# A Perceiver block on one core: self-attention of the first layer on row and column groups of the array, its softmax bank by bank, and the router's gates behind the first expert's products

## The chip, the cores and the metric

The kernel runs on one core of a Trainium2 chip. The metric is the device time in microseconds (us) of one execution, as the median of repeated runs. Engines are named as in the profile: PE is TensorE (PEld its weight loads), DVE is VectorE, ACT is ScalarE, POOL is GpSimd, SP is SyncE, which issues the DMAs. TensorE's clock has two levels, 1.2 and 2.4 GHz; the profile shows them as a granted clock of 0.50 and 1.00, called the lower and the upper level below.

## The reference, cut to what matters

128 tokens of width 256 pass through two layers. Each layer has cross-attention to 12,544 context rows, self-attention or a stand-in for it, and a mixture of experts. The change lies in the first layer, from the end of its cross-attention to its experts:

```python
x = x + cross_attention(layernorm(x), ctx)      # 16 heads of 16, then relu(out @ W1 + b1) @ W2 + b2
# self-attention, 16 heads of 16
q, k, v = split(layernorm(x) @ c_attn_w + c_attn_b)
w = q @ k.T / sqrt(16)                           # per head
w = softmax(where(causal, w, -1e10))
x = x + (w @ v) @ c_proj_w + c_proj_b
# 8 experts, the two best by softmax(x @ Wg + bg)
for e in range(8):
    x = x + (gelu(xn @ W1[e] + b1[e]) @ W2[e] + b2[e]) * w_e
```

## The kernel before, in words

Each engine runs its own list of instructions in the order in which the code issues them; waits on semaphores tie the lists together. `Settle` is a helper that makes DVE wait for its own last instruction. Nothing is planned at run time.

The first cross-attention walks the context twice: a first pass with 14 chunks of 896 rows makes keys, values and a maximum per query, a second pass with 98 steps scores, exponentiates and weighs. The second pass already uses column groups of the array: `weigh0` writes 32 columns of output at PSUM partitions 32*i for i in 0..3, 16 products to a step. The first pass uses row groups of 64: `score_pair` takes partitions 0 to 63 and 64 to 127 of its operands by turns.

Then comes a stage in which one engine after another works on 128 x 256 values (lines 916 to 981 of `tensor`, 1215 to 1228 of `scalar`, 1502 to 1546 of `vector`). `att` is transposed (`PE_AT`), DVE adds a bias (`D_AT`), PE makes the hidden layer (`PE_HID`), DVE its relu (`D_HID`), PE the output and its bias row (`PE_FFN`), DVE adds it to x. A layernorm follows (DVE, with one operation on POOL), its transpose (PE) and a copy (ACT, `xnT`). Self-attention projects queries and keys (`PE_QK`) and values (`PE_V`). DVE adds biases and spreads each query over the 128 partitions with a mask (`D_SPREAD`, 128 x 2048), so that each head's scores are one product over all 128 rows, of which 16 hold its query. PE puts the causal mask into a bank as a product with the identity and adds four heads' scores to it, four times (`PE_SC`). DVE takes one maximum over all heads and subtracts it (2048 columns each), ACT exponentiates all 2048 columns (`A_EXP`), PE transposes 16 heads, ACT and DVE copy a half each (`A_PT`, `D_PT`). PE then weighs with the probabilities as stationary operand and 16 columns of values as moving one (`PE_AV`), DVE multiplies by the reciprocal of the sums, PE transposes, ACT copies, PE projects (`PE_PR`).

The router (`gate`, 16 short DVE operations and one exponential) comes after the next layernorm. PE waits for it, turns the gates, waits for the copy on ACT, forms the gated bias `b2`, and only then starts `hidden0(0)`. The expert loop alternates `hidden0(e)` (16 products of 128 columns) and `down0(e-1)` (8 of 256). A loader on SP brings expert e+4 once expert e is summed.

Matrix products whose operands are float32 show as two records each in the profile. `mm` and DVE's and ACT's helpers put most records on the helper's line (L692, L1287, L1288, L1291, L1091), so groups are told apart by tile and shape. `q_all` in a row is also the scratch space of this stage.

Of the kernel before, what the change touches and what calls it, by code (L numbers as in the profile page):

```python
# [7 lines left out]
F32 = mybir.dt.float32  # L8
F16 = mybir.dt.float16
ALU = mybir.AluOpType  # L10
# [31 lines left out]
def perceiver_kernel(nc, d, out):  # L42
# [18 lines left out]
    with ExitStack() as ctx:  # L61
# [21 lines left out]
        cp = tail[:, 272:784].rearrange("p (a n) -> p a n", a=2)  # L83
        bias_rows = tail[0:8, 784:784 + D]
        wv16 = sb("wv16", [P, 4, 1024], F16)
        v16 = sb("v16", [P, 2 * 8 * 130], F16)
        W = sb("W", [P, 15680], F32)
# [17 lines left out]

        def dram(name, shape, dt=F16):
            return nc.dram_tensor(name, shape, dt, kind="Internal").ap()
# [5 lines left out]
        ld_ctx = [sem(f"ld_ctx{n}") for n in range(3)]  # L113
        ld_keys = [sem(f"ld_keys{n}") for n in range(2)]
# [4 lines left out]
        COLS_IN, TAIL_IN, GATE_IN = 6 * 16, 14 * 16, 16 * 16  # L119
# [28 lines left out]
        tail_blank = sem("tail_blank")  # L148
# [232 lines left out]
        qkT = scratch[:, 0:512].rearrange("p (a q) -> p a q", a=4)  # L381
        v_tok = scratch[:, 512:768]
        sa_spread = scratch[:, 768:768 + 2048].rearrange("p (h q) -> p h q", h=H)
        sa_probT = scratch[:, 768:768 + 2048].rearrange("p (h q) -> p h q", h=H)
        sa_prob = scratch[:, 2816:2816 + 2048].rearrange("p (h q) -> p h q", h=H)
# [10 lines left out]
        PE_AT, PE_HID, PE_FFN, PE_QK, PE_V, PE_SC, PE_PT, PE_AV, PE_AT2, PE_PR = range(1, 11)  # L396
        PE_WT, PE_B2, PE_WO, PE_VS, PE_VT, PE_VY = range(11, 17)
        A_VTOK, A_EXP, A_PT, A_AT2, A_WT, A_VEXP, A_VT = range(1, 8)
        D_AT, D_HID, D_SPREAD, D_CENTRED, D_PT, D_ATT, D_VCEN, D_VROWS = range(1, 9)


        def sync(sp):
# [95 lines left out]
            load_blocks(ld_bias, tail[:, 272:784], d["L0_attn_c_proj_w"])  # L498
# [7 lines left out]
            load_blocks(ld_w2, W[:, CA_OFF:], d["L0_attn_c_attn_w"])  # L506

# [182 lines left out]
        def tensor(pe):  # L690
# [231 lines left out]
            ins.then_inc(step_pe, 1)  # L922
            pe.wait_ge(step_dve, D_AT)
# [4 lines left out]
            ins.then_inc(step_pe, 1)  # L928
            pe.wait_ge(step_dve, D_HID)
            for f in range(4):  # L930
                mm(ps[:, 2, 0:D], ff_hT[:, f, :], w2[:, f, :], f == 0, False)
            mm(ps[:, 2, 0:D], row_select("L0_xattn_b2"), bias_rows, False, True).then_inc(step_pe, 1)


            turn_xn(1, 0)
            ca = wview(CA_OFF, 2, 3 * D)
            pe.wait_ge(ln_made, 2)
            for n in range(4):
                for a in range(2):
                    ins = mm(ps[:, 1, n * P:(n + 1) * P], ca[:, a, n * P:(n + 1) * P], xnT[:, a, :], a == 0, a == 1)  # L940
            ins.then_inc(step_pe, 1)
            for a in range(2):
                mm(ps[:, 2, 0:D], xnT[:, a, :], ca[:, a, 2 * D:3 * D], a == 0, False)
            mm(ps[:, 2, 0:D], row_select("L0_attn_c_attn_b"), bias_rows, False, True).then_inc(step_pe, 1)
            pe.wait_ge(step_dve, D_SPREAD)
            for b in range(4):
                mm(ps[:, 4 + b, :], ident[:, :], bc(causal[:, :], 1, [P, 4, P]), True, False, skip_group_check=True)
                for j in range(4):
                    h = 4 * b + j
                    ins = mm(ps[:, 4 + b, j * P:(j + 1) * P], sa_spread[:, h, :], qkT[:, 2 + h // 8, :], False, True,  # L950
                             skip_group_check=True)
            ins.then_inc(step_pe, 1)
            pe.wait_ge(step_act, A_EXP)
            for h in range(H):
                ins = pe.transpose(ps[:, h // 4, (h % 4) * P:(h % 4 + 1) * P], sa_prob[:, h, :], ident[:, :])
            ins.then_inc(step_pe, 1)
            pe.wait_ge(step_act, A_PT)
            pe.wait_ge(step_dve, D_PT)
            for h in range(H):
                ins = mm(ps[:, 4, h * 16:(h + 1) * 16], sa_probT[:, h, :], v_tok[:, h * 16:(h + 1) * 16], True, True)  # L960
            ins.then_inc(step_pe, 1)
            pe.wait_ge(step_dve, D_ATT)
            for i in range(2):
                ins = pe.transpose(ps[:, 5, i * P:(i + 1) * P], att[:, i * P:(i + 1) * P], ident[:, :])
            ins.then_inc(step_pe, 1)
            pe.wait_ge(step_act, A_AT2)
            for a in range(2):
                mm(ps[:, 6, 0:D], sa_attT[:, a, :], cp[:, a, :], a == 0, False)
            mm(ps[:, 6, 0:D], row_select("L0_attn_c_proj_b"), bias_rows, False, True).then_inc(step_pe, 1)


            turn_xn(2, 0)
            pe.wait_ge(ln_made, 3)
            for a in range(2):
                mm(ps[:, 1, 0:NE], xnT[:, a, :], wg[:, a, :], a == 0, False)
            mm(ps[:, 1, 0:NE], row_select("L0_ffn_bg"), bias_rows[:, 0:NE], False, True).then_inc(gate_in, 1)
            pe.wait_ge(gate_made, 1)
            pe.transpose(ps[0:8, 2, 0:P], g_w, ident[:, :]).then_inc(step_pe, 1)
            pe.wait_ge(step_act, A_WT)
# [658 lines left out]
```

## Time and profile before

| | |
|---|---|
| median of 3 runs | 1517.76 us (1512.5 to 1522.74) |
| the profiled execution, its own time | 1513.2 us |
| its span | 1511.5 us |
| PE busy / DVE busy / ACT busy | 1386.6 / 1042.2 / 1062.0 us |
| mean granted TensorE clock | 0.966 |
| second pass of the first cross-attention ends | 462.2 us |
| stage that the change touches | 462.2 to 586.8 us |

Times in the rows are microseconds from the start of the span. A timeline row gives start, duration from the first start to the last end, engine, line, operation, output <- inputs, shape, how many instructions, and in brackets how long the engine stood idle before it and what ended that.

### The profile page before, as it was taken

The page shows a single profiled execution, that of the slowest core. Times are in us where ns is not written, and L with a number is a line of the kernel's source. Part 1 is how long each engine was busy: PE and PEld are TensorE (multiplying, and loading weights), DVE is VectorE, ACT ScalarE, POOL GpSimd, SP SyncE. Part 2 cuts the span into 40 slices and gives each one's busy share as a digit, 9 for nine tenths or more (in the row PEclk, how much of TensorE's full clock was granted, in tenths as well). Part 3 has the DMA queues.
Part 4 walks back from the last instruction along what each step waited for, and adds up shares of the span by engine and source line. Part 5 has one row for each costly group of instructions (what it writes and reads, how often), then busy time and mean ns, then how long its engine had stood idle before and what let it go on. Part 6 is the DMA issues. An engine that isn't in the chain of part 4 may idle for free.

```text
span 1511.5 us, 36970 instructions
## 1 busy us (share of the span) xinstructions
PE 1386.6 (92%) x15312; PEld 921.4 (61%) x15312; DVE 1042.2 (69%) x1482; ACT 1062.0 (70%) x1630; POOL 106.4 (7%) x145
## 2 busy tenths in 40 slices
PE   5888887999997598999999979999998999989969
PEld 2444444777775497433333447777776777767758
DVE  6999997000002302999999998888888888887842
ACT  4787776999992133666666658888887888877820
POOL 6232220000000002200000000000000000000000
PEclk9999999999998599999999989999999999999979
DMA  4445437676656054555654567777777677797630
GB/s 138 157 183 185 168 121 200 155 181 148 170 127 223 1 196 136 191 183 201 229 192 179 188 148 147 147 146 146 147 139 146 123 147 143 147 258 136 158 125 4
DMA packets 128794, 236.48 MB, mean 156 GB/s; under 512 B 9244, under 2 KB 114166, under 8 KB 128630
## 3 DMA queue, kind: packets, MB, share of 16 engines
q1 hardware_dynamic: 128630, 234.13, 58.2%
q8 instruction: 122, 2.00, 0.6%
q14 instruction: 42, 0.34, 0.1%
HBM read 155.98 MB, written 78.12 MB: 155 GB/s over the span
## 4 chain that ended last, share of the span: by engine, by line
PE 61%; DVE 21%; issue 11%; ACT 2%; DMA 2%; SPq 2%; POOL 0%; POOLq 0%; DVEq 0%; ACTq 0%
PE ps L692 60%; DVE W L1291 6%; DVE small L1354 5%; DVE p L1291 5%; DMA W<-keys_hi 1%; SPq L405 1%; ACT W L1114 1%; DMA W<-in_ctx_dram 1%; DVE W L1321 1%; DVE q_all L1291 1%; SPq L463 0%; ACT p L1128 0%; DVE ctxT_b L1343 0%; DVE att L1291 0%; DVE ctxT_a_lo L1347 0%
## 5 line engine op out<-in xcount | busy, mean ns | idle before, releaser
L1291 DVE TENSOR_TENSOR p<-ps,p 128x512 f16<-128x512 f32 (+1 forms) x467 | 350.5, 751 | 70.2 <-ACT ps L1091 67.5
L1091 ACT ACTIVATE p<-ps 128x512 f16<-128x512 f32 (+1 forms) x490 | 329.2, 682 | 90.2 <-PE ps L692 88.0
L692 PEld LDWEIGHTS ps<-q_all,W 128*128 128x128 f16 (+1 forms) x3544 | 230.9, 99 | 69.7 <-issue 17.3
L692 PE MATMUL ps<-q_all,W 128*128 128x128 f16 (+2 forms) x3544 | 264.2, 227 | 9.1 <-DMA W<-keys_hi 6.1
L1354 DVE TENSOR_REDUCE small<-ps 128x1 f32<-128x896 f32 x224 | 241.4, 1079 | 4.7 <-PE ps L692 4.3
L1091 ACT ACTIVATE ps<-ps 128x512 f32<-128x512 f32 x392 | 235.8, 602 | 0.0
L692 PE MATMUL ps<-v,p 128*128 128x130 f16 x3136 | 169.7, 206 | 5.4 <-DVE p L1291 3.3
L692 PE MATMUL ps<-wv,ctxT_a_hi 128*128 128x512 f16 (+1 forms) x588 | 155.3, 346 | 10.3 <-DVE W L1321 6.1
L692 PEld LDWEIGHTS ps<-v,p 128*128 128x128 f16 x3136 | 147.4, 97 | 12.2 <-ACT ps L1091 3.6
L692 PE MATMUL ps<-wv,ctxT_b 128*128 128x512 f16 (+1 forms) x588 | 154.5, 344 | 0.0
L1291 DVE TENSOR_TENSOR v<-ps,v 128x512 f16<-128x512 f32 x196 | 135.4, 691 | 15.6 <-ACT v L1186 2.9
L1411 DVE COPY att<-ps 128x512 f32<-128x512 f32 x1 | 0.7, 692 | 204.4 <-PE ps L692 204.4
L692 PE MATMUL ps<-ctxT_a_hi,q_all 128*128 128x448 f16 (+1 forms) x464 | 126.3, 356 | 0.6 <-DVE p L1291 0.6
L692 PE MATMUL ps<-ctxT_b,q_all 128*128 128x448 f16 (+1 forms) x464 | 125.1, 353 | 0.0
L692 PE MATMUL ps<-W,q_all 64*128 64x448 f16 (+1 forms) x684 | 105.4, 363 | 19.1 <-DVE small L1354 6.6
L1116 ACT CAST p<-ps 128x896 f16<-128x896 f32 x75 | 68.0, 906 | 61.0 <-PE ps L692 61.0
L692 PE MATMUL ps<-wv,ctxT_a_lo 128*128 128x512 f16 (+1 forms) x294 | 101.3, 344 | 0.0
L1091 ACT ACTIVATE W<-ps 128x1024 f32<-128x1024 f32 x98 | 95.0, 1021 | 7.4 <-PE ps L692 5.1
L1128 ACT CAST p<-ps 128x896 f16<-128x896 f32 x104 | 92.9, 907 | 9.9 <-PE ps L692 8.9
L692 PEld LDWEIGHTS ps<-wv,ctxT_b 128*128 128x128 f16 x588 | 57.6, 98 | 48.9 <-issue 0.8
L692 PE MATMUL ps<-ctxT_a_lo,q_all 128*128 128x448 f16 (+1 forms) x240 | 82.7, 354 | 0.0
L692 PEld LDWEIGHTS ps<-W,q_all 64*128 64x128 f16 (+1 forms) x684 | 35.7, 108 | 70.6 <-issue 38.7
(226 smaller groups left out, 1744.8 us busy)
## 6 DMA issues: line engine op xcount, KB each, us to landing
W<-keys_hi SPq DMA_DIRECT2D x54, 896.0 KB, 14.6
W<-keys_low SPq DMA_DIRECT2D x27, 896.0 KB, 11.7
keys_hi<-p SPq DMA_DIRECT2D x75, 224.0 KB, 2.0
keys_low<-p SPq DMA_DIRECT2D x75, 224.0 KB, 1.9
keys_hi<-W SPq DMA_DIRECT2D x65, 224.0 KB, 2.0
keys_low<-W SPq DMA_DIRECT2D x65, 224.0 KB, 2.0
W<-values SPq DMA_DIRECT2D x14, 960.0 KB, 9.2
W<-in_L_ffn_W_dram SPq DMA_DIRECT2D x10, 1024.0 KB, 8.8
```

The lines of the kernel that those rows point to most:

```text
L405: sp.dma_start(by_rows(region, a, n), src.rearrange("(a p) n -> p a n", p=P)).then_inc(s, 16)
L692: return pe.matmul(out_, lhsT, rhs, start=start, stop=stop, **kw)
L1091: return act.activation(out_, in_, ACT.Exp, scale=scale)
L1114: ins = act.activation(dst, src, ACT.Identity, bias=bk_scaled[:, i:i + 1])
L1116: ins = act.copy(dst, src)
L1128: act.copy(dst.rearrange("p (n k) -> p n k", n=MAXB), src).then_inc(max_copied, 1)
L1291: return dve.tensor_tensor(out_, a, b, op)
L1321: ins = dve.scalar_tensor_tensor(out=low, in0=src, scalar=bk_scaled[:, i:i + 1], in1=hi, op0=ALU.add, op1=ALU.subtract)
L1354: dve.tensor_reduce(mpart[:, among(L, h), n:n + 1], ps[:, 2 * pair:2 * pair + 2, 0:MAXC], AX.XY, ALU.max).then_inc(max_reduced, 1)
L1411: dve.tensor_copy(att[:, 512:1024], ps[:, O0_BANK, :]).then_inc(outT_made, 1)
```

## The change

Order of PE's list and what it computes with:

- The four causal products leave the score loop: they are issued behind the transposes of `att`, behind the hidden layer, and two behind the FFN output. The bias rows of the FFN output, of the value projection, of the output projection and of the router's logits are issued ahead of the wait that their product had, as the first of the group.
- Queries and keys go to two banks. DVE writes each query twice, scaled by 0.25 and by `quarter`, a 0/0.25 mask of every other 16 rows (`q_half`); ACT adds the keys' bias (`kT`). Scores are products over 32 partitions, four row groups by turns, each into its own bank.
- The softmax goes bank by bank: DVE maximum and subtraction of 512 columns, ACT exponential of 512, PE four transposes, ACT (three banks) or DVE (the last) copy of 512.
- The values (32 columns of `v_tok`, the last 16 rows of zeros from a memset) are the stationary operand, the probabilities the moving one, over four column groups, like `weigh0`; a same set with a block of ones before it gives the sums, spread over the partitions. DVE takes the reciprocal of 128 x 512 sums. The result is already transposed, so the transposes, their copy and the separate scaling are gone. The projection takes four products with a `cp` that is zero in every other 16 rows. It lies in the space of `wv16`, blanked by DVE and loaded by four DMAs behind the loads of the FFN's weights.
- The gates' transpose is issued behind `hidden0(0)`, the gated bias behind `hidden0(1)`; ACT copies the gates behind the first expert's gelu.

```diff
+            def add_causal(r):
+                mm(ps[:, 4 + r, :], ident[:, :], bc(causal[:, :], 1, [P, 4, P]), True, False, skip_group_check=True)
+            add_causal(0)
             pe.wait_ge(step_dve, D_AT)
...
+            mm(ps[:, 2, 0:D], row_select("L0_xattn_b2"), bias_rows, True, False)
+            add_causal(1)
             pe.wait_ge(step_dve, D_HID)
...
+            add_causal(2)
+            add_causal(3)
             turn_xn(1, 0)
+            mm(ps[:, 2, 0:D], row_select("L0_attn_c_attn_b"), bias_rows, True, False)
             pe.wait_ge(ln_made, 2)
...
-            pe.wait_ge(step_dve, D_SPREAD)
-            for b in range(4):
-                mm(ps[:, 4 + b, :], ident[:, :], bc(causal[:, :], 1, [P, 4, P]), True, False, skip_group_check=True)
-                for j in range(4):
-                    h = 4 * b + j
-                    ins = mm(ps[:, 4 + b, j * P:(j + 1) * P], sa_spread[:, h, :], qkT[:, 2 + h // 8, :], False, True,
+            pe.wait_ge(step_dve, D_Q)
+            pe.wait_ge(step_act, A_K)
             for a in range(2):
+                for j in range(2):
+                    for r in range(4):
+                        rows, n = slice(32 * r, 32 * (r + 1)), 2 * a + j
+                        ins = mm(ps[:, 4 + r, n * P:(n + 1) * P], q_half[rows, j, a, :], kT[rows, a, :], False, True,
...
+            for r in range(4):
+                pe.wait_ge(sa_exped, r + 1)
+                for n in range(4):
+                    ins = pe.transpose(ps[:, r, n * P:(n + 1) * P], sa_prob[:, 4 * r + n, :], ident[:, :])
+                ins.then_inc(sa_turned, 1)
+            pe.wait_ge(sa_copied, 3)
+            pe.wait_ge(step_dve, D_PT)
+            for bank in (4, 5):
+                for k in range(4):
+                    for i in range(4):
+                        h = 4 * k + i
+                        lhsT = ones32 if bank == 4 else v_tok[:, h * 16:h * 16 + 32]
+                        ins = mm(ps[32 * i:32 * (i + 1), bank, k * P:(k + 1) * P], lhsT, sa_probT[:, sa_slot(h), :],
+                                 True, True)
+                ins.then_inc(step_pe, 1)
+            mm(ps[:, 6, 0:D], row_select("L0_attn_c_proj_b"), bias_rows, True, False)
+            pe.wait_ge(ld_cp, 64)
+            pe.wait_ge(step_dve, D_ATT)
+            for k in range(4):
+                ins = mm(ps[:, 6, 0:D], sa_out[:, k * P:(k + 1) * P], cp[:, k, :], False, k == 3)
...
-            pe.wait_ge(gate_made, 1)
-            pe.transpose(ps[0:8, 2, 0:P], g_w, ident[:, :]).then_inc(step_pe, 1)
-            pe.wait_ge(step_act, A_WT)
-            mm(ps[:, 1, 0:D], wT, bias2, True, True).then_inc(step_pe, 1)
...
                 if e < NE:
                     hidden0(e)
+                if e == 0:
+                    pe.wait_ge(gate_made, 1)
+                    pe.transpose(ps[0:8, 0, 0:P], g_w, ident[:, :]).then_inc(step_pe, 1)
+                if e == 1:
+                    pe.wait_ge(step_act, A_WT)
+                    mm(ps[:, 1, 0:D], wT, bias2, True, True).then_inc(step_pe, 1)
                 if e:
                     down0(e - 1)
...
+            act.wait_ge(step_pe, PE_K)
+            for a in range(2):
+                ins = act.activation(kT[:, a, :], ps[:, 3, a * P:(a + 1) * P], ACT.Identity,
+            for r in range(4):
+                act.wait_ge(sa_centred, r + 1)
+                own = sa_prob[:, 4 * r:4 * (r + 1), :]
+                exp(own, own).then_inc(sa_exped, 1)
+                if r:
+                    act.wait_ge(sa_turned, r)
+                    act.copy(sa_probT[:, 4 * (r - 1):4 * r, :].rearrange("p n q -> p (n q)"), ps[:, r - 1, :]).then_inc(sa_copied, 1)
...
+                dve.wait_ge(values0_out, 4 * NCH)
+                dve.memset(cp, 0.0).then_inc(cp_blank, 1)
...
+            for a in range(2):
+                for j in range(2):
+                    ins = ts(q_half[:, j, a, :], ps[:, 1, a * P:(a + 1) * P], col("L0_attn_c_attn_b", a),
+                             quarter[:, j:j + 1], ALU.add, ALU.mult)
...
+            for r in range(4):
+                scores = ps[:, 4 + r, :].rearrange("p (n q) -> p n q", n=4)
+                own = mx[:, 4 * r:4 * (r + 1)]
+                settle(dve.tensor_reduce(own, scores, AX.X, ALU.max))
+                tt(sa_prob[:, 4 * r:4 * (r + 1), :], scores, bc(own, 2, [P, 4, P]), ALU.subtract).then_inc(sa_centred, 1)
+            dve.wait_ge(sa_turned, 4)
+            dve.tensor_copy(sa_probT[:, 12:16, :].rearrange("p n q -> p (n q)"), ps[:, 3, :]).then_inc(step_dve, 1)
+            dve.wait_ge(step_pe, PE_SUM)
+            settle(dve.reciprocal(per_sum, ps[:, 4, :]))
+            dve.wait_ge(step_pe, PE_AV)
+            tt(sa_out, ps[:, 5, :], per_sum, ALU.mult).then_inc(step_dve, 1)
```

PE's list from the transposes of `att` to the first expert; `causal` is the mask, `stage,ident` a bias row, `q_all` stands for the scratch. Before:

```order
L921 MATMUL ps<-ident,att 128x128 x2
L692 MATMUL ps<-q_all,W 128x128 x8
L692 MATMUL ps<-W,q_all 128x256 x4
L692 MATMUL ps<-stage,ident 128x256
L696 MATMUL ps<-ident,xn 128x128
L697 MATMUL ps<-ident,xn 128x128
L692 MATMUL ps<-xnT,W 128x128 x8
L692 MATMUL ps<-W,xnT 128x256 x2
L692 MATMUL ps<-stage,ident 128x256
L692 MATMUL ps<-causal,ident 128x512
L692 MATMUL ps<-q_all 128x128 x4
```

and in the changed kernel:

```order
L936 MATMUL ps<-ident,att 128x128 x2
L707 MATMUL ps<-causal,ident 128x512
L707 MATMUL ps<-q_all,W 128x128 x8
L707 MATMUL ps<-stage,ident 128x256
L707 MATMUL ps<-causal,ident 128x512
L707 MATMUL ps<-W,q_all 128x256 x4
L707 MATMUL ps<-causal,ident 128x512 x2
L711 MATMUL ps<-ident,xn 128x128
L712 MATMUL ps<-ident,xn 128x128
L707 MATMUL ps<-stage,ident 128x256
L707 MATMUL ps<-xnT,W 128x128 x8
L707 MATMUL ps<-W,xnT 128x256 x2
```

The mask stands in three places ahead of the scores, and each bias row ahead of its products.

PE's list from the weighing to the first expert's products (`small` holds the block of ones and the gates, `wv` the projection's weights). Before:

```order
L692 MATMUL ps<-q_all 128x16 x16
L964 MATMUL ps<-ident,att 128x128 x2
L692 MATMUL ps<-stage,q_all 128x256 x2
L692 MATMUL ps<-stage,ident 128x256
L696 MATMUL ps<-ident,xn 128x128
L697 MATMUL ps<-ident,xn 128x128
L692 MATMUL ps<-stage,xnT 128x8 x2
L692 MATMUL ps<-stage,ident 128x8
L978 MATMUL ps<-ident,small 8x128
L692 MATMUL ps<-stage,q_all 128x256
L692 MATMUL ps<-xnT,stage 128x128 x16
```

and in the changed kernel:

```order
L707 MATMUL ps<-q_all,small 32x128 x16
L707 MATMUL ps<-q_all,att 32x128 x16
L707 MATMUL ps<-stage,ident 128x256
L707 MATMUL ps<-wv,q_all 128x256 x4
L711 MATMUL ps<-ident,xn 128x128
L712 MATMUL ps<-ident,xn 128x128
L707 MATMUL ps<-stage,ident 128x8
L707 MATMUL ps<-stage,xnT 128x8 x2
L707 MATMUL ps<-xnT,stage 128x128 x16
L1042 MATMUL ps<-ident,small 8x128
```

The gates' transpose has moved behind the 16 products of the first expert.

## Rows read from the trace of the kernel before

**Rows 1.** The page: the chain that ended last, shares of the span by engine
```profile
PE 61%; DVE 21%; issue 11%; ACT 2%; DMA 2%; SPq 2%; POOL 0%; POOLq 0%; DVEq 0%; ACTq 0%
```

**Rows 2.** Stretches: from:to, length, PE busy (x records), granted clock, DMA share, GB/s
```profile
465.00:475.00 10.00, 8.08 (x27) 0.50 1.06 383
479.00:482.00 3.00, 2.99 (x14) 0.52 1.04 382
482.00:495.00 13.00, 9.18 (x50) 1.00 0.14 44
496.00:533.00 37.00, 23.48 (x91) 0.50 0.00 1
533.00:587.00 54.00, 53.80 (x362) 1.00 0.56 190
```

**Rows 3.** Timeline, FFN output to the scores
```profile
462.26 0.69 DVE L1411 COPY att<-ps 128x512 f32<-128x512 f32 x1 [204.43 <-PE ps L692]
466.00 3.78 PE L692 MATMUL ps<-q_all,W 128*128 128x128 f32 x16 [0.70 <-DVE q_all L1287]
471.00 3.78 PE L692 MATMUL ps<-W,q_all 128*128 128x256 f32 x8 [1.22 <-DVE q_all L1288]
475.59 0.42 DVE L1291 TENSOR_TENSOR x_tok<-ps,x_tok 128x256 f32<-128x256 f32 x1 [4.65 <-PE ps L692]
479.01 3.40 PE L692 MATMUL ps<-xnT,W 128*128 128x128 f32 x16 [0.46 <-ACT xnT L1095]
486.03 1.12 PE L692 MATMUL ps<-causal,ident 128*128 128x512 f32 x2 [2.13 <-DVE q_all L1291]
486.99 1.05 PE L692 MATMUL ps<-q_all 128*128 128x128 f32 x8
```

**Rows 4.** Timeline, softmax to the projection
```profile
493.34 2.29 DVE L1531 TENSOR_REDUCE small<-ps 128x16 f32<-128x2048 f32 x1 [7.36 <-PE ps L692]
499.95 3.68 PE L955 MATMUL ps<-ident,q_all 128*128 128x128 f32 x16 [6.65 <-ACT q_all L1091]
505.11 6.98 PE L692 MATMUL ps<-q_all 128*128 128x16 f32 x32 [1.48 <-DVE q_all L1538]
517.01 0.42 DVE L1291 TENSOR_TENSOR x_tok<-ps,x_tok 128x256 f32<-128x256 f32 x1 [4.46 <-PE ps L692]
```

**Rows 5.** Timeline, the router and the first experts
```profile
520.59 1.02 PE L692 MATMUL ps<-stage,xnT 128*128 128x8 f32 x4 [0.46 <-ACT xnT L1095]
525.68 0.23 DVE L1287 TENSOR_SCALAR small<-small 128x8 f32<-128x8 f32 x1
527.84 6.32 PE L692 MATMUL ps<-xnT,stage 128*128 128x128 f32 x32
541.03 3.73 PE L692 MATMUL ps<-xnT,W 128*128 128x128 f32 x32
544.60 3.62 PE L692 MATMUL ps<-W,q_all 128*128 128x256 f32 x16
```

**Rows 6.** Groups by shape: busy us, mean ns of one; ACT, DVE, reciprocals
```profile
L1091 ACT ACTIVATE ps<-ps 128x512 f32<-128x512 f32 x392 | 235.8, 602 | 0.0
L1291 DVE TENSOR_TENSOR q_all<-ps,q_all 128x512 f32<-128x512 f32 x8 | 5.5, 691 | 24.0 <-PE ps L692 24.0
L1431 DVE RECIPROCAL small<-small 128x3 f32<-128x3 f32 x4 | 0.7, 176 | 0.1
L1416 DVE RECIPROCAL small<-small 128x16 f32<-128x16 f32 x1 | 0.3, 253 | 0.0
```

**Rows 7.** Timeline: column groups in the second pass, row groups in the first
```profile
445.52 0.81 PEld L692 LDWEIGHTS ps<-W 128*32 128x32 f32 x32 [0.21 <-issue]
445.52 1.08 PE L692 MATMUL ps<-W 128*32 128x128 f32 x32
120.86 0.11 PEld L692 LDWEIGHTS ps<-W,q_all 64*128 64x128 f16 x4 [0.37 <-DVE W L1321]
120.86 0.55 PE L692 MATMUL ps<-W,q_all 64*128 64x448 f16 x4
```

More of the change, by code:

```diff
@@ L104, in perceiver_kernel @@
         bk_scaled = small[:, 234:236]
+        quarter, ones32 = small[:, 48:50], small[:, 64:96]
         def dram(name, shape, dt=F16):
@@ L935, in tensor @@
+            add_causal(2)
+            add_causal(3)
             turn_xn(1, 0)
             ca = wview(CA_OFF, 2, 3 * D)
+            mm(ps[:, 2, 0:D], row_select("L0_attn_c_attn_b"), bias_rows, True, False)
             pe.wait_ge(ln_made, 2)
-            for n in range(4):
-                for a in range(2):
-                    ins = mm(ps[:, 1, n * P:(n + 1) * P], ca[:, a, n * P:(n + 1) * P], xnT[:, a, :], a == 0, a == 1)
+            for bank, first in ((1, 0), (3, 2)):
+                for n in range(2):
+                    w = slice((first + n) * P, (first + n + 1) * P)
+                    for a in range(2):
+                        ins = mm(ps[:, bank, n * P:(n + 1) * P], ca[:, a, w], xnT[:, a, :], a == 0, a == 1)
+                ins.then_inc(step_pe, 1)
@@ L956, in tensor @@
-            ins.then_inc(step_pe, 1)
[L957 to L965, printed above, removed]
@@ L976, in tensor @@
[L976 to L980 removed]
+                ins = mm(ps[:, 1, 0:NE], xnT[:, a, :], wg[:, a, :], False, a == 1)
+            ins.then_inc(gate_in, 1)
             def hidden0(e):
@@ L1194, in attend1 @@
                             exp(bank, bank, 1.0 / VS).then_inc(exped, 1)
-            def copy_attT(n, dst, bank, value):
-                nb = -(-n // 4)
-                w = min(n, 4) * P
-                act.wait_ge(step_pe, value)
-                return act.copy(dst.rearrange("p (b i) q -> p b (i q)", b=nb), ps[:, bank:bank + nb, 0:w])
             def gate(k, second):
@@ L1441, in attend0 @@
                 first_pass(L0)
+                dve.wait_ge(values0_out, 4 * NCH)
+                dve.memset(cp, 0.0).then_inc(cp_blank, 1)
+                settle(dve.tensor_reduce(quarter, head16[:, :].rearrange("p (a j) -> p j a", j=2), AX.X, ALU.add))
+                ts(quarter, quarter, 0.25, None, ALU.mult)
+                dve.memset(ones32, 1.0)
                 normalise0()
@@ L1517, in vector @@
             layernorm(1)
-            dve.wait_ge(step_pe, PE_QK)
-            for n in range(4):
-                ins = ts(qkT[:, n, :], ps[:, 1, n * P:(n + 1) * P], col("L0_attn_c_attn_b", n),
-                         0.25 if n < 2 else 1.0, ALU.add, ALU.mult)
-            settle(ins)
-            for i in range(2):
-                ins = tt(sa_spread[:, 8 * i:8 * i + 8, :], bc(qkT[:, i, :], 1, [P, 8, P]),
-                         bc(head16[:, :], 2, [P, 8, P]), ALU.mult)
+            dve.memset(v_tok[:, D:D + 16], 0.0)
@@ L1526, in vector @@
+            dve.wait_ge(step_pe, PE_Q)
+            for a in range(2):
+                for j in range(2):
+                    ins = ts(q_half[:, j, a, :], ps[:, 1, a * P:(a + 1) * P], col("L0_attn_c_attn_b", a),
+                             quarter[:, j:j + 1], ALU.add, ALU.mult)
             ins.then_inc(step_dve, 1)
-            mx, tot = small[:, 16:32], small[:, 32:48]
-            sch = ps[:, 4:8, :].rearrange("p b (j q) -> p b j q", j=4)
-            mx4 = mx.rearrange("p (b j) -> p b j", b=4)
+            mx = small[:, 16:32]
```

80 lines of the change are left out of this document (35 added, 45 removed).

## The prediction

> **What bounds the kernel now.** I read the chain of waits first: by engine PE holds 61% of it, DVE 21%, "issue" 11% [rows 1]. Over the whole span that says little about this change, so the next view is the stage itself, 462.2 to 586.8 us. In the chain's order of time every piece there follows the one before within 0.02 to 0.14 us, on alternating engines: nothing overlaps until the first expert. So here each microsecond taken from the chain comes off the time. The timeline gives the pieces: FFN [rows 3], scores [rows 3], softmax, weighing and projection [rows 4], router [rows 5]. Then the stretches with the granted clock [rows 2]: 0.50 from 465 to 475, 1.00 from 482 to 495, 0.50 from 496 to 533, 1.00 in the experts. At the lower level a float32 product of 256 columns costs 3.78/4 = 0.95 us, at the upper 3.62/8 = 0.45; one of 128 columns 3.40/8 = 0.42 mostly at the lower, 3.73/16 = 0.23 at the upper [rows 3, 5]. The clock rose after PE had worked without a pause for some 3 to 6 us (from 471.0 it rose by 475, from 479.0 by 482, from 527.8 at 533), and it was low again in the stage wherever PE mostly waited.
>
> **The change, term by term** (times of before in brackets; negative is gain).
>
> a) To the FFN's residual [its wait ends at 475.59]. The first mask product begins as the last transpose of `att` streams, 0.9 us before the hidden layer's 466.00. Masks cost 486.99 - 486.03 = 0.96 us each at the upper level [rows 3], twice that at the lower. The wait for DVE was only 0.70 us, so the hidden layer starts about 1 us later than 466.00. But PE now has no gap from 464.7 on; I expect the clock to rise some 3 to 4 us in, which makes the hidden layer's 3.78 about 2.6 and ends it near 469.5 (before 469.78). DVE's relu takes 1.13; under it go the bias row (0.45) and the second mask (0.96), about as long. The four output products cost 4 x 0.45 = 1.8 plus 0.1 to drain: residual at 472.6. **-3.0**. Of this, 0.84 is the bias row off the path, the rest the clock.
>
> b) To the first score product [475.59 to 486.03, masks not counted]. Layernorm to xn is unchanged, 2.5 us, and covers masks three and four (1.9 at the upper level, 3.6 at the lower). Transposes and the copy to xnT 0.9; the value bias row hides under the copy. Then PE runs 8 products of 128 columns (8 x 0.23 = 1.9) and 2 of 256 (0.9). Queries are ready halfway: DVE's four operations (1.1) end before the values do, and ACT's two (0.37 each, as its copies of 256 columns) with them. What goes: the wait for the queries' bias behind all eight products and the spread over 128 partitions, 2.4 us of DVE. 2.5 + 0.9 + 1.9 + 0.9 = 6.2 against 10.4. **-4.2**.
>
> c) Scores [486.03 to 493.32, 7.3]. Masks gone: 4 x 0.9. The 16 products took 16 x 0.23 = 3.6. In row groups they fall between two bounds. Above: nothing overlaps, 3.6. Below: four groups at once, 3.6/4 = 0.9 plus a drain of 0.15. The nearest row is the first pass's two groups of 64: four products of 448 columns took 0.55 us, where one alone streams 0.187, and their four weight loads took 0.11 together [rows 7]. Both loads and products overlap there, so I take 1.05. **-6.2**. The Trainium skill, "TensorE: Matmul & The Clock Gate", Part 3, gives 3.07x for four row groups; by it this would be 3.6/3.07 = 1.2 us, an estimate. No row here has four row groups or float32 ones.
>
> d) Softmax to the first weighing product [493.34 to 505.11, 11.8]. DVE does per bank a maximum and a subtraction, each a quarter of 2.29 with its fixed part, 0.62 [rows 4], at most 0.69 [rows 6]; the fourth bank is centred after 8 x 0.64 = 5.1 us, 0.5 more than now. But ACT (0.60 + 0.60 per bank [rows 6]) and PE (four transposes 3.68/4 = 0.92 at the lower level [rows 4]) keep pace with its 1.28. After the fourth: exponential 0.6, transposes 0.95, DVE's copy 0.69, hand-offs 0.1: 7.45 in all. **-4.3**. The sum over probabilities and its reciprocal of 16 (2.5 us on DVE) were hidden by PE and don't count.
>
> e) Weighing to the residual [505.11 to 517.01, 11.9]. Before, 6.98 for 16 products of 16 columns (at the lower level, bound by weight loads), scaling 0.44, transposes 0.70, copy 0.38, projection 3.2. Now two sets of 16 in column groups: 1.08 each at the upper level, the very form of the second pass [rows 7], 2.15 at the lower. The reciprocal of 128 x 512 is on the path behind the first set. From 3 to 16 columns it rises 77 ns, 5.9 ns a column [rows 6], so 512 cost 3.2; a bound below is 0.69, as any operation on 512 [rows 6]. I take 3.2, since the slope is measured on the same instruction; it hides the second set. Scaling 0.69, four products 3.7 or 1.9. 2.15 + 3.2 + 0.7 + 3.7 + 0.15 = 9.9 at the lower level, 8.1 if the weighing, over 4 us without a pause, lifts the clock. I take 9.0. **-2.9**. The Trainium skill, "VectorE: DVE Perf Modes", in the walkthrough of the pipeline's modes, says that a reciprocal repeats its divide step 8 times, at 0.96 GHz; by it 512 columns would be 4.3 us, an estimate, and the time 1.1 us longer. The slope of the rows is less.
>
> f) Router [520.59 to 527.84, 7.25]. Now the experts' products follow the logits' four records (1.0) at once. DVE's gates, whose last operation ends 525.91 - 521.61 = 4.3 us behind them [rows 5], lie beside the first 16 products, 6.3 at the lower level and 3.7 at the upper: no or next to no wait. The gates' transpose (0.25) and the gated bias (0.45) now stand between full products. -6.25 + 0.7 = **-5.5**. The copy of the gates on ACT is due while `hidden0(1)` runs, after the first gelus; covered.
>
> Edits at nothing: `memset`s, `quarter` and the blanking of `cp` fall into the 204 us in which DVE waits for the second pass [rows 3]; the four small loads go out 200 us before their use, and SP's wait for the blanking ends before the next keys are wanted. The loads that run at 479 to 482 (DMA share 1.04) are the weights of experts 1 and 3; they are nearly over in the next stretch (0.14) [rows 2], and needed from about 508. Later loads are released by the experts themselves and move along, as all behind does.
>
> **Sum**: 3.0 + 4.2 + 6.2 + 4.3 + 2.9 + 5.5 = 26.1 us. On the profiled execution's 1513.2 that is 1487.1; the median shown is 4.6 higher, so 1491.7. I forecast **1491**.
>
> A switch of the array's form may cost too. In the second pass, which switches twice a step, the weight loader stands 0.21 us at each switch [rows 7], and PE doesn't show it. The Trainium skill, "TensorEngine Tiling (Array Packing)", Key Properties, says that changing the mode drains TensorE; by it the four new switches would add about 4 x 0.2 = 0.8 us, an estimate with the row's length.
>
> **Rivals.**
> 1. *The clock stays at the lower level until the scores.* For: from 465 to 475 PE was busy for 8.08 of 10 us and the clock stayed there [rows 2]. Against: the two rises that came within 4 us. Then a) is +1.3 (a mask of 1.9 in a gap of 0.7, mask and bias row of 2.8 in one of 1.2, less the bias row), b) -1.8, c) -5.2, e) -2.0: gain 17.5, time 1500. Chance 0.15.
> 2. *Float32 row groups don't overlap*, by loads of 128 columns each. c) is -3.7, the time 1494. Chance 0.13.
> 3. *Hand-offs eat it*: the softmax ping-pong waits at every bank and the change is within 1%. That needs 11 us more than worked out, on some 30 hand-offs of 0.02 to 0.14 us each. Chance 0.04.
> 4. *Slower: the experts run at the lower level.* Before, the clock rose only after 5 us of unbroken products from 527.84. Now the experts start from the same low clock, with a wait for the gates that could break the run. An expert costs 7.0 us at the upper level [rows 5], twice that at the lower. To eat 26 us and cost 15 more, six of eight experts would have to run low: 1517.8 + 16 = 1534. Against it: PE had no pause of a microsecond in its 54 us [rows 2]. Chance 0.02.
>
> The forecast itself keeps 0.66. The range takes in the cheap reciprocal and a clock that is high throughout (-2.5, -2.5, and 3 for the spread of runs) and the first rival: **1483 to 1502**. A measurement tells about 1% from no change, 15 us; below 1502.6 is faster. All of forecast and rival 2, and two thirds of rival 1, lie there: faster 0.89, same 0.09, slower 0.02.
>
> **What would show it.** Hidden layer ends within 0.5 us of where it did and the FFN's products take under 2 us; 16 score products in a little over 1 us; the sums' reciprocal near 3.2 us, with PE idle behind the weighing for it; x's second residual some 20 us earlier; first expert's products within 1 us of the logits; experts as long as before. I am wrong if scores take over 3 us, if the clock shows 0.50 from 465 to the scores, if the softmax takes over 9 us from scores to weighing, or if the stretches outside the stage change length.

## The result and the profile after

The changed kernel takes 1493.39 us (median of 4 runs, 1491.6 to 1495.53) against 1516.15 for the kernel before (the median of four runs now; of the first three it was 1517.76): ratio 0.9848, 95% interval 0.9824 to 0.9872, 22.8 us less. The profiled execution's span went from 1511.5 to 1490.9 us, by 20.6. The forecast was 1491, the range 1483 to 1502. Two executions of kernels further down, 1631.39 us of the one with only the gates' part and 3298.05 us of the one with products in the stage, were slow ones and stand in no ratio.

Timeline of the changed kernel, attention output to the first score's maximum; columns as in [rows 3]:

```profile
467.63 0.44 PE L936 MATMUL ps<-ident,att 128*128 128x128 f32 x2 [1.01 <-DVE att L1330]
467.90 1.72 PE L707 MATMUL ps<-causal,ident 128*128 128x512 f32 x2
469.41 2.95 PE L707 MATMUL ps<-q_all,W 128*128 128x128 f32 x16
473.88 1.89 PE L707 MATMUL ps<-W,q_all 128*128 128x256 f32 x8
475.81 0.42 DVE L1330 TENSOR_TENSOR x_tok<-ps,x_tok 128x256 f32<-128x256 f32 x1 [2.28 <-PE ps L707]
479.32 2.05 PE L707 MATMUL ps<-xnT,W 128*128 128x128 f32 x16
482.18 1.17 PE L707 MATMUL ps<-q_all 32*128 32x128 f32 x32
483.41 0.69 DVE L1574 TENSOR_REDUCE small<-ps 128x4 f32<-128x512 f32 x1 [1.52 <-PE ps L707]
```

The output products of the FFN take 1.89 us where they took 3.78 [rows 3], queries and keys 2.05 instead of 3.40. All scores take 1.17 us, with no mask between them. Each DVE operation on 512 columns takes 0.69.

The same view from the last bank's copy to the first expert:

```profile
490.66 0.69 DVE L1577 COPY q_all<-ps 128x512 f32<-128x512 f32 x1 [1.87 <-PE ps L985]
491.50 1.93 PE L707 MATMUL ps<-q_all,small 128*32 128x128 f32 x32 [0.88 <-DVE q_all L1577]
493.18 1.96 PE L707 MATMUL ps<-q_all,att 128*32 128x128 f32 x32
493.49 3.36 DVE L1579 RECIPROCAL q_all<-ps 128x512 f32<-128x512 f32 x1 [2.14 <-PE ps L707]
497.72 2.69 PE L707 MATMUL ps<-wv,q_all 128*128 128x256 f32 x8 [1.81 <-DVE q_all L1330]
500.44 0.42 DVE L1330 TENSOR_TENSOR x_tok<-ps,x_tok 128x256 f32<-128x256 f32 x1 [2.87 <-PE ps L707]
504.01 1.03 PE L707 MATMUL ps<-stage,xnT 128*128 128x8 f32 x4
504.89 5.80 PE L707 MATMUL ps<-xnT,stage 128*128 128x128 f32 x32
```

PE stands idle 1.81 us ahead of the projection: first the reciprocal (493.49 to 496.85), then the scaling. The first expert's products begin 0.88 us behind the first of the logits', before it was 7.25 [rows 5].

Measured from the same marks, term by term:

| term | before | after | gain | forecast |
|---|---|---|---|---|
| a) transposes of att to the FFN's residual | 10.91 | 8.18 | 2.7 | 3.0 |
| b) residual to the scores or their masks | 10.44 | 6.37 | 4.1 | 4.2 |
| c) scores and masks | 7.31 | 1.23 | 6.1 | 6.2 |
| d) first maximum to the first weighing product | 11.77 | 8.09 | 3.7 | 4.3 |
| e) weighing to the residual | 11.90 | 8.94 | 3.0 | 2.9 |
| f) logits to the experts, less 0.4 in the experts | 7.25 | 1.28 | 6.0 | 5.5 |
| sum | | | 25.5 | 26.1 |

So the stage gave 25.5 us and the span 20.6. In these two profiles the rest was given back outside. POOL does one short operation in every layernorm, which marks the places. In the kernel before, those of the layernorms ahead of self-attention and behind the experts:

```profile
477.03 0.58 POOL L575 TENSOR_TENSOR small<-small,minus_half 128x1 f32<-128x1 f32 x1 [248.13 <-DVE small L1287]
588.41 0.55 POOL L575 TENSOR_TENSOR small<-small,minus_half 128x1 f32<-128x1 f32 x1 [0.52 <-DVE small L1287]
```

In the changed kernel these two stand at 477.25 and 565.86: level at the first, 22.6 us ahead at the second. The next one (1448.65 before) is at 1427.79. From the experts' end to the second layer's self-attention that is 861.93 us instead of 860.24, 1.7 lost. Ahead of the stage 2.95 were lost: the transposes of att start at 467.63, where before they stood at 464.68.

```profile
464.68 0.61 PE L921 MATMUL ps<-ident,att 128*128 128x128 f32 x2 [1.01 <-DVE att L1291]
```

Of these, 0.6 stood there before the second pass began. Another 1.2 come from the clock at its start: the pass's second step begins at 262.31 before and at 264.11 after. The last 1.1 arise further on in the pass, in single waits at the upper level; no run shows why. Stretches (length, PE busy, granted clock) at the start, of before:

```profile
253.00:260.00 7.00, 3.69 (x16) 0.51 1.10 237
260.00:264.00 4.00, 4.00 (x82) 1.00 1.03 387
```

and of the changed kernel:

```profile
253.00:260.00 7.00, 3.11 (x14) 0.50 1.10 235
260.00:264.00 4.00, 4.00 (x46) 0.59 1.04 385
```

In both PE is busy throughout 260 to 264; one has the upper level there, the other mostly the lower, and gets 46 records done instead of 82. The change does nothing to PE in this place.

How much of this is the change's doing can be read from the other profiles. With the code of before up to here, the second pass's last products start at 461.12 (this profile) and 464.12 (the kernel with only the gates' part). With the change's code and no further edit ahead of the stage they start between 463.93 and 467.23, in nine profiles. So the 2.95 lie within what profiles of the same code differ by; whether the change itself costs a microsecond or two there is not settled. Behind the stage, between the same two layernorms, those nine take 858.90 to 863.64 us, the two with the older code 860.24 and 861.55: no loss is shown there.

### The profile page after: what moved, and what is told of

It is laid out like the page before. It is cut to its first block, busy times and chain, and to the rows that moved or that the text cites. A ratio compares the mean times of both kernels' runs of the same rounds, so it can differ in the third digit from the quotient of the medians.

```text
span 1490.9 us, 37058 instructions
## 1 busy us (share of the span) xinstructions
PE 1380.0 (93%) x15346; PEld 913.6 (61%) x15346; DVE 1042.3 (70%) x1490; ACT 1063.4 (71%) x1636; POOL 106.3 (7%) x145
## 4 chain that ended last, share of the span: by engine, by line
PE 61%; DVE 22%; issue 11%; ACT 2%; SPq 2%; DMA 2%; POOL 0%; POOLq 0%; DVEq 0%; ACTq 0%
PE ps L707 60%; DVE W L1330 6%; DVE small L1393 6%; DVE p L1330 5%; DMA W<-keys_hi 1%; SPq L417 1%; ACT W L1151 1%; DVE W L1360 1%; DVE q_all L1330 1%; DVE ctxT_b L1382 0%; DMA W<-in_ctx_dram 0%; SPq L475 0%; ACT p L1165 0%; DVE att L1330 0%; DVE ctxT_a_lo L1386 0%
## 5 line engine op out<-in xcount | busy, mean ns | idle before, releaser
L707 PEld LDWEIGHTS ps<-ctxT_a_hi,q_all 128*128 128x128 f16 (+1 forms) x464 | 37.7, 101 | 67.1 <-DVE p L1330 30.8
```

The costliest lines, as they stand in the source:

```text
L707: return pe.matmul(out_, lhsT, rhs, start=start, stop=stop, **kw)
```

## The experiments

Each kernel was timed in 5 rounds against the kernel before unless it says otherwise. A job is one sitting on one chip. The first held the change once more, both kernels with moved gates and the one with products in the stage; the second held late masks, scores row group by row group, the softmax in one piece and the reciprocal in halves; the third the other three. Differences between kernels of different jobs are differences of medians, good to 2 or 3 us; what rests on less is read from the traces.

**The change once more**, as yardstick.

> The changed kernel once more, as the yardstick for the three beside it. Every theory expects about 22 us under the kernel before (ratio 0.985) and the stage from the transposes of att to the last expert some 25 us shorter than before.

1493.88 us, ratio 0.9859 (0.9842 to 0.9876). In its trace the two layernorms around self-attention are 25.64 us apart, against 24.56 in the first profile and 41.35 before. So one profile of the very same kernel differs from another by 1 us in this stage. Its rows show that single terms differ by more:

```profile
469.27 0.44 PE L936 MATMUL ps<-ident,att 128*128 128x128 f32 x2 [1.01 <-DVE att L1330]
470.41 2.05 PE L707 MATMUL ps<-q_all,W 128*128 128x128 f32 x16
475.90 0.42 DVE L1330 TENSOR_TENSOR x_tok<-ps,x_tok 128x256 f32<-128x256 f32 x1 [2.28 <-PE ps L707]
497.82 3.75 PE L707 MATMUL ps<-wv,q_all 128*128 128x256 f32 x8 [1.43 <-DVE q_all L1330]
```

Here the clock did not fall ahead of the hidden layer, which takes 2.05 instead of 2.95, and term a) is 6.63 us, a gain of 4.3. The projection lies wholly at the lower level, 3.75 instead of 2.69, and term e) is 10.01, a gain of 1.9. From the transposes of att to the layernorm behind the experts it is 97.74 us, 98.23 in the first profile and 123.73 before: the sum repeats, its two clock-dependent terms do not.

**Gates ahead of the experts again.**

```diff
             ins.then_inc(gate_in, 1)
+            pe.wait_ge(gate_made, 1)
+            pe.transpose(ps[0:8, 0, 0:P], g_w, ident[:, :]).then_inc(step_pe, 1)
+            pe.wait_ge(step_act, A_WT)
+            mm(ps[:, 1, 0:D], wT, bias2, True, True).then_inc(step_pe, 1)
...
-                if e == 0:
-                    pe.wait_ge(gate_made, 1)
-                    pe.transpose(ps[0:8, 0, 0:P], g_w, ident[:, :]).then_inc(step_pe, 1)
-                if e == 1:
-                    pe.wait_ge(step_act, A_WT)
-                    mm(ps[:, 1, 0:D], wT, bias2, True, True).then_inc(step_pe, 1)
```

> The changed kernel with the gates' transpose and the gated bias put back ahead of the first expert. Theory (terms of the prediction add up): the experts' first product stands 7.0 us behind the first logits' product again, where it was 0.9, less 0.7 for the two products that leave the loop: 5.5 us slower than the change, ratio to the kernel before 0.988 to 0.990. Rival (the gain of the gates depends on the clock: with PE idle for the gates the first expert starts at the lower level either way, so the rise of the clock moves too): up to 3 us more or less than 5.5. Rival (other engines would have covered it): under 2 us.

1499.51 us, 5.6 more than the yardstick in the same job; ratio 0.9897 (0.988 to 0.9914). From PE's timeline:

```profile
504.69 1.02 PE L707 MATMUL ps<-stage,xnT 128*128 128x8 f32 x4
509.56 0.38 PE L1013 MATMUL ps<-ident,small 128*8 128x128 f32 x1 [3.84 <-DVE small L1323]
510.28 1.22 PE L707 MATMUL ps<-stage,q_all 8*128 8x256 f32 x2 [0.34 <-ACT q_all L1264]
511.43 4.00 PE L707 MATMUL ps<-xnT,stage 128*128 128x128 f32 x17
```

The experts begin 6.7 us behind the logits, 3.84 of them a wait for DVE's gates. The theory's 5.5 holds.

**Only the gates' part, on the kernel before** (the same edit the other way round).

> The kernel before with only the gates' part of the change. Theory: 5.5 us faster than before, ratio 0.996, the experts' first product right behind the logits. If the parts lean on each other (the gates only pay off when self-attention is short), under 2 us, ratio 0.999 or more.

1511.05 us, ratio 0.9964 (0.995 to 0.9977), 5.5 us less than before in the same job. Layernorm to layernorm around the experts: 64.06 us, 70.03 before, 64.05 in the change. Term f) is independent of the rest.

**The masks put back ahead of the scores.**

```diff
-            add_causal(0)
...
-            add_causal(1)
...
-            add_causal(2)
-            add_causal(3)
...
             pe.wait_ge(step_act, A_K)
+            for r in range(4):
+                add_causal(r)
```

> The changed kernel with the four mask products put back right ahead of the scores. Theory (the early masks gain twice: 3.9 us off the path ahead of the scores, and a PE without pauses from the transposes of att on, which lifts the clock in the hidden layer): the clock shows 0.50 from 465 to 475 as in the kernel before, the FFN's output products take 3.8 us instead of 1.9, and the kernel is 5 to 7 us slower than the change. Rival (the clock's early rise was the bias row's or chance): only 3.9 us slower, output products 1.9.

1498.59 us, ratio 0.9896 (0.9867 to 0.9924), 4.7 above the yardstick of the other job, just under the 5 to 7 expected. From PE's timeline:

```profile
469.24 2.66 PE L707 MATMUL ps<-q_all,W 128*128 128x128 f32 x16 [0.70 <-DVE q_all L1324]
473.12 3.78 PE L707 MATMUL ps<-W,q_all 128*128 128x256 f32 x8
480.45 3.55 PE L707 MATMUL ps<-xnT,W 128*128 128x128 f32 x16
484.84 3.64 PE L707 MATMUL ps<-causal,ident 128*128 128x512 f32 x8
```

The output products are back at 3.78, queries and keys at 3.55, and the masks cost 3.6 in the path. The expectation missed one thing: the clock was not at 0.50 throughout 465 to 475, its mean there was 0.77, so the hidden layer took 2.66, no more than in the change. The kernel with only the gates' part, which has the code of before here, shows 2.68. So the hidden layer's own time does not tell the two orders apart; the output products and what follows do.

**Masks late, but unread products of the same shape in their old places.** `fill` is identity by mask into a free bank, 512 columns:

```diff
+            fill(7, 512)
             pe.wait_ge(step_dve, D_AT)
...
             mm(ps[:, 2, 0:D], row_select("L0_xattn_b2"), bias_rows, True, False)
+            fill(7, 512)
...
+            fill(7, 512, 2)
             turn_xn(1, 0)
```

> The kernel with late masks, and at the three places where the change has its masks as many products of the same shape whose result nobody reads. The scores' path is the longer one of masks_late (masks 3.6 us ahead of the scores), PE's occupation ahead of it that of the change. Theory (the early masks gain by leaving the path and, separately, by keeping PE without a pause): the FFN's output products take 1.9 us again and queries and keys 2.05, as in the change, and only the masks' 3.6 us stay lost: 1 to 3 us faster than masks_late in spite of the added work. Rival (the clock's course there is chance): same as masks_late or slower.

1495.46 us, ratio 0.9861 (0.9845 to 0.9878), 3.1 less than without them, though PE does four more products. The two are of different jobs, so the traces decide. From its timeline:

```profile
474.05 1.89 PE L707 MATMUL ps<-W,q_all 128*128 128x256 f32 x8
479.49 2.05 PE L707 MATMUL ps<-xnT,W 128*128 128x128 f32 x16
482.35 3.67 PE L707 MATMUL ps<-causal,ident 128*128 128x512 f32 x8
```

Output products and projections are at the change's speed again, granted clock 1.00 from 465 to 475, and only the masks' 3.7 remain. This parts term a) and b) from c): in those, part of the gain is the clock that PE gets when its waits are filled, whatever fills them. The rival, chance, falls by the count of profiles: the output products take 3.78 us in all three without products in those waits and 1.89 in all ten with them, queries and keys 3.40 to 3.55 against 2.05.

**Scores row group by row group** (one execution, 1496.21 us; `for r` outermost instead of innermost).

> The changed kernel with the 16 score products ordered row group by row group (four in a row in the same 32 partitions) instead of by turns. Theory (the gain in the scores is that products of different row groups run at once, which needs them next to each other): the products take 2.5 to 3.7 us instead of 1.17. Rival (a product over 32 partitions is simply quicker, or PE overlaps across its whole queue): 1.2 us as in the change.

```profile
485.34 2.62 PEld L707 LDWEIGHTS ps<-q_all 32*128 32x128 f32 x32 [0.33 <-DVE q_all L1327]
485.35 2.80 PE L707 MATMUL ps<-q_all 32*128 32x128 f32 x32
```

The same 16 products take 2.80 us when four in a row use the same partitions and 1.17 when they go by turns, a factor of 2.4. So the order by turns gives most of the gain, and rival 2 of the prediction falls. Of the 2.4 us that the products gained over the 3.6 of before, 1.6 hang on the order. The other 0.8 are there without it, which this run's own rival (a product over 32 partitions is simply quicker) had in part. By turns each product also goes to another bank than the one before it; no run parts that from the row groups. For column groups different banks are not needed: the 16 sum products, all into one bank, take 1.08 in the kernel with filled waits below. The Trainium skill, "TensorE: Matmul & The Clock Gate", Part 3, gives 3.07x for four row groups; against one product after another over all 128 rows, 3.6 us here, the change has 3.1.

**Softmax in one piece**: one maximum, subtraction and exponential over 2048 columns, copies of 1024.

> The changed kernel with the softmax in one piece again: one maximum and one subtraction over 2048 columns, one exponential, 16 transposes, copies of 1024 by ACT and DVE. Theory: from the end of the scores to the first sum 2.3 + 2.3 + 1.9 + 3.7 + 1.3 = 11.6 us instead of 8.1, so 3.5 us slower than the change. Rival (the 17 hand-offs and the fixed part of each small instruction eat the overlap): under 1.5 us slower.

1496.77 us, ratio 0.9871 (0.9848 to 0.9893). From the first maximum (483.29) to the first sum product (495.05) it takes 11.76 us, in the change 8.09: 3.7 slower, as worked out; by the medians, of different jobs, 2.9. Against the rival, the hand-offs behind the change's last bank cost 0.03, 0.06, 0.03 and 0.15 us, about what they cost before.

**The reciprocal in halves**: sums of heads 8 to 15 in bank 7, each half of 256 columns as soon as it is summed.

```diff
+                        own = 7 if bank == 4 and k >= 2 else bank
...
+                    if bank == 4 and k == 1:
+                        ins.then_inc(half_summed, 1)
...
-            settle(dve.reciprocal(per_sum, ps[:, 4, :]))
+            dve.wait_ge(half_summed, 1)
+            dve.reciprocal(per_sum[:, 0:256], ps[:, 4, 0:256])
+            dve.wait_ge(step_pe, PE_SUM)
+            settle(dve.reciprocal(per_sum[:, 256:512], ps[:, 7, 256:512]))
```

> The changed kernel with the sums of heads 0 to 7 in one bank and 8 to 15 in another, and the reciprocal of each half of 256 columns taken as soon as its half is summed. Theory (the reciprocal is on the path and costs 6.4 ns a column): it begins 0.9 us sooner, two of 1.7 us back to back, the projection starts 0.8 us sooner. Rival (DVE's reading and PE's writing of PSUM get in each other's way, or the weighing becomes the bound): no gain.

```profile
492.35 1.93 PE L707 MATMUL ps<-q_all,small 128*32 128x128 f32 x32 [0.88 <-DVE q_all L1580]
493.49 1.76 DVE L1582 RECIPROCAL q_all<-ps 128x256 f32<-128x256 f32 x1 [1.28 <-PE ps L707]
495.16 1.70 DVE L1584 RECIPROCAL q_all<-ps 128x256 f32<-128x256 f32 x1
497.73 1.97 PE L707 MATMUL ps<-wv,q_all 128*128 128x256 f32 x8 [0.95 <-DVE q_all L1333]
```

From the first sum product to the projection's start 5.38 us, in the change 6.22: 0.84 gained, and the reciprocal is shown to be on the path. The time, 1491.93 us (ratio 0.9845, 0.982 to 0.987), does not settle a difference this small.

**Unread products where PE waits, in the stage**: two of 512 columns ahead of the first transposes, one of 256 behind each bank's, one and a half ahead of the projection, two behind it.

> The changed kernel with products whose result nobody reads (identity by mask, 256 or 512 columns, into a free bank) where PE waits: two ahead of the first transposes, one behind each bank's transposes, two ahead of the projection, two behind it. Theory (from scores to the first expert PE works at the lower level because it mostly waits): granted clock 1.00 from the scores on, transposes 0.5 us a bank, sums and weighing 1.08 each, projection 1.9, the first expert's products 3.7: 3 to 5 us faster than the change although PE does more. Rival (the clock does not follow PE's own products, or the fillers stand in the way in PE's order): same time or up to 4 us slower.

1487.27 us, ratio 0.9816 (0.9799 to 0.9834), 6.6 less than the yardstick in the same job. From PE's timeline:

```profile
491.40 1.08 PE L707 MATMUL ps<-q_all,small 128*32 128x128 f32 x32 [0.44 <-DVE q_all L1589]
492.27 1.08 PE L707 MATMUL ps<-q_all,att 128*32 128x128 f32 x32
493.91 1.56 PE L707 MATMUL ps<-causal,ident 128*128 128x512 f32 x4
496.68 1.99 PE L707 MATMUL ps<-wv,q_all 128*128 128x256 f32 x8 [1.21 <-DVE q_all L1342]
```

Granted clock 1.00 from 480 to 500, where the change has 0.71; sums and weighing 1.08 each as expected. Transposes took 0.65 a bank instead of 0.5. The first expert's products took 5.44 instead of 3.7, at a granted clock of 0.72 from 502 to 508. The two profiles' spans differ by 7.4 us. Of these the stage has 4.2: layernorm to layernorm 22.47 us (yardstick 25.64), around the experts 63.04 (64.03). Another 2.9 lie in the second layer (859.13 against 862.01), which the edit does not touch; two kernels without such products, scores row group by row group and halves, have 858.90 and 859.60 there. So about 4 us are shown to be the products' work, the middle of what was expected; that the rest is theirs is not.

**The same outside the stage**, with the change inside it: 4 and 7 products in the waits at the end of the two first passes, and 1, 2, 2, 3, a half and 2 further on.

```diff
+                if L is L0:
+                    pe.wait_ge(max_reduced, max(v for k, v in N_RED.items() if k[0] == 0))
+                    pe.wait_ge(max_copied, max(v for k, v in N_COP.items() if k[0] == 0))
+                    pe.wait_ge(values0_out, 4 * NCH)
+                    fill(6, 512, 4)
+                else:
+                    pe.wait_ge(keys_low, L.k0 + L.nB)
+                    fill(0, 512, 7)
                 pe.wait_ge(shift_made, L.n + 1)
-                if L is L0:
-                    pe.wait_ge(values0_out, 4 * NCH)
```

The waits ahead of `shift_made` stand before the added products, so that these run while PE would wait for the shift.

> The changed kernel with such unread products outside the stage only: in the waits at the end of both first passes (4 and 7 of 512 columns, and 1 ahead of the second pass), ahead of the transposes behind the experts (2), and in the second layer's last stages (2, 3, a half, 2). Theory (after each of these waits PE works 3 to 17 us at the lower level): the low stretches at 253, 567, 861 and from 1431 on shrink or go, 6 to 10 us faster than the change. Rival (there other engines set the pace, so that PE's clock is idle gain): under 2 us.

1482.91 us, ratio 0.9774 (0.9755 to 0.9793), 11.0 below the yardstick of another job, a little more than expected. The stretch 861 to 875 in the change, and then with the products:

```profile
861.00:875.00 14.00, 6.27 (x33) 0.53 0.46 98
```

```profile
861.00:875.00 14.00, 13.09 (x170) 1.00 1.06 203
```

The two stretches do not hold the same work, since this kernel is 8.5 us ahead by then. Counted from the same instruction, the shift's transpose, the third weighing product of the pass comes 12.35 us later in the change and 11.08 in this kernel:

```profile
868.73 0.64 PE L707 MATMUL ps<-ident,small 128*32 128x128 f32 x2 [8.39 <-DVE small L1330]
881.08 0.86 PE L707 MATMUL ps<-v,p 128*128 128x130 f16 x16
```

```profile
860.24 0.41 PE L707 MATMUL ps<-ident,small 128*32 128x128 f32 x2 [1.72 <-DVE small L1347]
871.32 0.86 PE L707 MATMUL ps<-v,p 128*128 128x130 f16 x16
```

The clock stands at 1.00 there, at the start of the first layer's second pass (250 to 265), behind the experts (562 to 580) and from 1430 to 1450, where the change has 0.53, 0.66, 0.81 and 0.57.

Set beside the change's first profile, the span is 13.1 us shorter. By the same marks 2.2 lie at the start of the first layer's second pass, 2.9 between the experts and the second layer's shift, 1.3 behind that, 4.3 behind the last long pass (63.11 to 58.79 us). But 3.7 lie inside the first layer's second pass from its second step on (199.95 to 196.29 us), where nothing was added and both have 1.00 from 266 on. From 266 to 456, PE's waits put down to "issue" sum to 6.8 us in the change and 3.0 here. Elsewhere 1.3 are lost. Why the waits in that pass are shorter is not shown; a better clock in that stretch cannot be the cause.

**All together**: products inside and outside, reciprocal in halves.

> The changed kernel with the unread products inside the stage and outside it, and the reciprocal in halves. Theory (the gains add up, since each is on the path): filled -6.6, outside -6 to -10, halves -0.8: 1477 to 1481 us, ratio to the kernel before 0.975 to 0.978. Rival (filled had 3 of its 6.6 us from a later stage by chance of the clock's course, which can't be had twice): 1482 to 1485.

**1475.86 us**, ratio 0.9736 (0.9716 to 0.9756): 17.5 us under the change by the medians, 41 under the kernel before of its job (1517.0). A little below the lower end of what was expected, and close to 1493.88 - 6.6 - 11.0 - 0.8 = 1475.5, so the gains do add up. The added products are never read.

## Why the prediction was right, point by point

- *What bounds.* A chain without overlap: what a term takes out of the stage comes off the time. Shown by the gates, whose part is 5.5 us on the kernel before and 5.6 on the change, and by the masks and the softmax, which cost time when they are put back. The table's sum (25.5 of 26.1) shows that the stage was costed rightly. The time itself fell by 22.8, 3.3 short of the forecast. The forecast of 1491 came within 2.4 us also because the kernel before read 1.6 lower with its fourth run.
- *a)* 2.7 for 3.0. The mechanism was right, masks as cover and as work that lifts the clock; shown by the two kernels with late masks. That the size fits so well is partly luck of the two profiles: this term took 10.91 or 9.69 us with the code of before, 8.2 or 6.6 with the early masks, by where the clock fell. The hidden layer ended 4.7 us behind the start of the transposes of att instead of 4.8; the clock rose within it.
- *b) and c)* 4.1 and 6.1 for 4.2 and 6.2. Products by turns over row groups overlap in float32 too, 1.17 us for the 1.05 taken. The bound above, 3.6, was not reached even with the groups in sequence (2.80).
- *d)* The term that was mis-sized: 3.7 for 4.3, 8.09 us for 7.45. DVE's four banks took 5.38 for 5.1 (all eight operations took 0.68 or 0.69, the upper value that I had named, for 0.62), the last exponential 0.63 for 0.6, the last transposes 1.12 for 0.95, and the hand-offs behind the fourth bank 0.27 for 0.1.
- *e)* 3.0 for 2.9. The reciprocal took 3.36 us; the slope of the small ones [rows 6] had given 3.2, the end below (0.69) was far off. The Trainium skill, "VectorE: DVE Perf Modes", would have given an estimate of 4.3 by eight repeats of the divide step; the measurement decides, 6.4 ns a column between 256 (1.70 to 1.76 us) and 512. Weighing was at the lower level, and the projection, with 2.69, partly at the upper, so the value taken between the two levels fitted. That was luck: the same kernel's second profile has 3.75, and the term's gain is 1.9 there.
- *f)* 6.0 for 5.5; the experts never waited for the gates. The time up to the experts shrank by 6.4 for 6.25, and from their first product to the layernorm behind them it grew by 0.4 (60.57 to 60.97), not 0.7.
- *All behind moves along.* This step is the weak one. I had named a change of length outside the stage as a sign of being wrong, and there was one: 2.95 us ahead of the stage, 1.7 behind it. The traces show that the clock rises sooner or later after PE's waits there, from one profile to the next, with the same instructions, and that profiles of the same code differ by 3 us ahead of the stage and nearly 5 behind it. So the sign was set finer than single profiles can tell. Why the medians moved 2.7 less than the table's sum is open. They show more than the profiled spans (22.8 against 20.6) because the profiled execution of before, 1513.2 us, lies 3 us under its median and that of the change, 1492.63, only 0.8.
- *Rivals.* The clock did not stay low until the scores; the row groups overlap; hand-offs took 0.03 to 0.15 us each; the experts ran at the upper level from 510 on. None of the four came about. The first was priced 0.7 too low: a mask of 1.9 in a gap of 0.7 and 2.8 of work in one of 1.2, less the bias row's 0.84, make +2.0 for a), not +1.3.

## What to carry to other kernels

In a stretch where engines take turns, write down the chain piece by piece and cost an edit by the pieces that it removes; the sum came out within 3% here, though the two terms that hang on the clock differed by 1.1 and 1.6 us between two profiles of one kernel. Whatever has no input to wait for (masks, bias rows, the next block's first products) belongs into the wait ahead of its place, and pays twice if it keeps PE from pausing. Where PE waits several microseconds and then has a burst of work on the path, products that nobody reads brought 17 us more, a few of them not by the clock of the same stretch; look for stretches at a granted clock of 0.5 in which PE is busy.

## What had not been expected of the hardware

- Products of 32 partitions in the same row group, one after another, took 0.175 us each (2.80/16), less than the 0.23 of a product over 128 partitions with the same columns. Whether they still overlap in part, or each is quicker, is not shown.
- The reciprocal's cost per column is nearly the same from 3 columns to 512: 5.9 ns by the small ones, 6.4 between 256 and 512.
- Unread products made the kernel faster by 11 us outside the stage without taking any instruction off the path. Part of it, 3.7 us in the profile, came where the clock was already at the upper level.
